# Eight-stage network on one core: an order written out as turns, softplus and decays kept in PSUM, one scan per state tile, double-width GpSimd products, stage 4's weights laid over the convolutions'

## The reference

```python
x = _layernorm(x + _L0_attn_ref(x, ...))   # stage 0: Mamba mixer and MLP
x = _layernorm(x + _L0_ffn_ref(x, ...))    # stage 1: 16-head attention, then 7 experts
x = _layernorm(x + _L1_attn_ref(x, ...))   # stage 2: linear attention
x = _layernorm(x + _L1_ffn_ref(x, ...))    # stage 3: MLP with binarized weights
x = _layernorm(x + _L2_attn_ref(x, ...))   # stage 4: 16-head attention
x = _layernorm(x + _L2_ffn_ref(x, ...))    # stage 5: 8 experts
x = _layernorm(x + _L3_attn_ref(x, ...))   # stage 6: attention with a pruned context
x = _layernorm(x + _L3_ffn_ref(x, ...))    # stage 7: 8 experts and a shared one
```

```python
xs, zs = jnp.split(jnp.einsum('bld,ed->ble', x, in_proj_w), 2, axis=-1)
u  = jax.nn.silu(conv(xs)); zc = jax.nn.silu(conv(zs))
dt, Bm, Cm = jnp.split(jnp.einsum('bld,ed->ble', u, x_proj_w), [...], axis=-1)
delta = jax.nn.softplus(jnp.einsum('blr,dr->bld', dt, dt_proj_w) + dt_proj_b)
dA = jnp.exp(delta * A)          # decays, A = -exp(A_log)
dBu = delta * Bm * u
h = dA_t * h + dBu_t             # scan over the tokens
y = einsum(h, Cm) + u * Dp
x = x + einsum(concat(y, zc), out_proj_w)
x = x + gelu(ln(x) @ w1 + b1) @ w2 + b2
```

## Time and profile before

| | |
|---|---|
| median of 3 runs | 1385.8 us |
| the profiled execution, its own time | 1385.3 us |
| its span, first to last instruction | 1383.5 us |
| TensorE busy | 1280.2 us (93%) |
| VectorE busy | 941.4 us (68%) |
| ScalarE busy | 896.0 us (65%) |
| GpSimd busy | 789.7 us (57%) |
| mean granted TensorE clock | 0.968 |
| DMA, mean | 49 GB/s |

### The profile page before, as it was taken

How to read it: one execution, slowest core, us unless ns; L and a number is a source line. 1 busy time by engine, 2 the same in 40 slices (tenths; PEclk the granted TensorE clock), 3 DMA queues, 4 the chain that set the end, 5 groups by cost and what they waited for, 6 DMA issues and landing times.

```text
span 1383.5 us, 26286 instructions
## 1 busy us (share of the span) xinstructions
PE 1280.2 (93%) x8734; PEld 909.6 (66%) x8734; DVE 941.4 (68%) x3661; ACT 896.0 (65%) x2495; POOL 789.7 (57%) x876
## 2 busy tenths in 40 slices
PE   8577988899977889999999999999999999999997
PEld 4233655567644666677767867777777867886665
DVE  5989868677568677757563663485988659864253
ACT  6736689787474679767787676556568664775231
POOL 2998666576378556466556756355435325450534
PEclk9868899899998999999999999999999999999999
DMA  8742000101141100110010001301020030001431
GB/s 285 193 122 76 9 9 2 55 2 55 55 103 28 37 1 1 55 65 1 1 63 1 1 1 63 125 1 62 2 81 1 1 93 1 2 2 70 115 91 32
DMA packets 23109, 67.86 MB, mean 49 GB/s; under 512 B 2336, under 2 KB 9120, under 8 KB 20672
## 3 DMA queue, kind: packets, MB, share of 16 engines
q1 hardware_dynamic: 22976, 66.20, 15.2%
HBM read 62.85 MB, written 3.34 MB: 48 GB/s over the span
## 4 chain that ended last, share of the span: by engine, by line
PE 65%; DVE 11%; POOL 9%; ACT 8%; issue 5%; DMA 2%; SPq 0%; POOLq 0%; DVEq 0%; ACTq 0%
PE bank L1064 57%; PE bank L1068 8%; ACT arena L1514 6%; POOL arena L2315 3%; DMA arena<-cf 2%; DVE arena L1769 2%; DVE arena L2261 2%; POOL arena L2386 1%; DVE arena L2254 1%; DVE arena L2012 1%; POOL arena L2385 1%; POOL arena L2328 1%; DVE arena L1947 1%; DVE arena L2010 1%; DVE stats L1783 1%
## 5 line engine op out<-in xcount | busy, mean ns | idle before, releaser
L1514 ACT ACTIVATE arena<-arena 128x256 f32<-128x256 f32 (+4 forms) x808 | 357.9, 447 | 64.7 <-DVE arena L2012 32.5
L1514 ACT ACTIVATE arena<-bank 128x512 f32<-128x512 f32 (+3 forms) x355 | 190.7, 563 | 230.3 <-PE bank L1064 144.5
L1064 PE MATMUL bank<-XT,W 128*128 128x512 f32 (+1 forms) x752 | 290.2, 523 | 1.0 <-DVE arena L1775 0.6
L1064 PEld LDWEIGHTS bank<-W,arena 128*128 128x128 f32 x1888 | 231.5, 193 | 52.5 <-issue 39.4
L1064 PE MATMUL bank<-W,arena 128*128 128x128 f32 (+1 forms) x1888 | 243.4, 279 | 6.2 <-POOL arena L2328 3.1
L2385 POOL TENSOR_TENSOR arena<-arena 128x256 f32<-128x256 f32 x192 | 117.6, 613 | 220.8 <-DVE arena L2018 220.0
L1064 PE MATMUL bank<-arena 128*32 128x128 f32 (+8 forms) x2912 | 228.0, 336 | 16.2 <-ACT arena L1514 7.4
L2328 POOL TENSOR_TENSOR arena<-arena 128x512 f32<-128x512 f32 (+1 forms) x108 | 170.8, 1601 | 93.7 <-DVE arena L1769 39.0
L1064 PEld LDWEIGHTS bank<-arena 128*32 128x32 f32 (+4 forms) x2912 | 154.8, 153 | 81.1 <-issue 45.2
L1068 PE MATMUL bank<-CF,arena 128*128 128x128 f32 x1312 | 182.1, 279 | 23.9 <-POOL arena L2386 10.7
L2386 POOL TENSOR_TENSOR arena<-arena 128x512 f32<-128x512 f32 x192 | 199.7, 1040 | 0.0
(11 more groups left out here) (138 smaller groups left out, 1700.5 us busy)
## 6 DMA issues: line engine op xcount, KB each, us to landing
arena<-rws SPq DMA_DIRECT2D x8, 2048.0 KB, 7.4
arena<-rep SPq DMA_DIRECT2D x62, 256.0 KB, 5.9
arena<-rws SPq DMA_DIRECT2D x4, 1792.0 KB, 6.6
W<-w SPq DMA_DIRECT2D x2, 2124.0 KB, 8.6
arena<-rws SPq DMA_DIRECT2D x8, 384.0 KB, 10.4
W<-w SPq DMA_DIRECT2D x1, 2692.0 KB, 9.3
XT<-wkq SPq DMA_DIRECT2D x4, 512.0 KB, 8.3
W<-w SPq DMA_DIRECT2D x1, 2005.0 KB, 15.5
```

The lines of the kernel that those rows point to most:

```text
L1064: return e.matmul(o, lhsT, rhs, start=start, stop=stop, skip_group_check=True)
L1514: return e.activation(o, a, func, **kw)
```

## The change

It has seven parts.

1. The order is no longer computed by priorities. A table `TURNS` gives every part of every step a place in one sequence of about 3,900 (a negative number chooses the second of two engines); each engine's list is that sequence cut down to its parts. The tables `AHEAD`, `URGENT`, `HASTE` and `STAY` go.
2. Softplus works in the bank of `0.dt`: the exponential, the three corrections and delta itself stand in PSUM. A new ScalarE step `0.dc` copies delta to SBUF for `0.da`, without the first column of each sequence, which VectorE sets to zero. `0.da`'s exponentials leave that column out too, so that its decay is zero.
3. With a zero decay at the first token of each sequence, one scan runs over all 512 columns.
4. `0.db` multiplies two ring tiles in one GpSimd operation, 128x1024.
5. `0.da` repeats two tiles at a time in two banks, not four in four: eight groups a chunk for four. C stays in its bank until the last `0.ac`, and VectorE's `0.hc` reads it there; GpSimd still reads a copy in SBUF.
6. `0.b` and `0.x` go. b2 comes into `0.o`'s bank by four matmuls with one row, and `0.y` gets a second VectorE operation that leaves 2x + y where `0.o` adds.
7. Stage 0's weights change places, stage 4's go to columns 2087 to 4519, over the projections and taps, and its `load` waits for `0.in#1` and `0.dt` of all chunks, not for `0.e`. In addition, a `1.km` step is whole on ScalarE, or its second half on either engine.

```diff
-W_AT = {3: WMAX - 1160, 2: WMAX, 4: 2048}
+W_AT = {3: WMAX - 1160, 2: WMAX, 4: 4135}
...
-    loads = [("load", s, 0, [("f" if q else "0.e", 0, c, q) for q in OVER[s] for c in range(NC)]
+    loads = [("load", s, 0, [need for q in OVER[s] for c in range(NC) for need in ([("f", 0, c, q)] if q else [("0.in", 1, c, 0), ("0.dt", 0, c, 0)])]
...
+TURNS = {
+    ("0.n", 0, 0): (9, 13, 14, 16, 18), ("0.in", 0, 0): (25, 33, 53, 66), ("0.bc", 0, 0): (40, 47), ("0.dt", 0, 0): (43, 52, 59),
...
+        for p, (engines, one, other) in enumerate(x.parts):
+            turn = next(rows[x.name, x.s, x.c])
+            x.parts[p] = (engines[0], one) if turn > 0 else (engines[1], other)
+            turns[x.parts[p][0]].append((abs(turn), x, p))
...
+        def later(a):
+
+            return a.rearrange("p (b l) -> p b l", b=2)[:, :, 1:256]
...
                     act(s0(c, 12), bank[b.i][:, :], ACT.Abs, bias=wt(0, "dtb")).then_inc(has["sf_a"], 1)
...
-                    act(s0(c, 13), s0(c, 12), ACT.Exp, scale=-1.0).then_inc(has["sf_e"], 1)
+                    act(bank[b.i][:, :], s0(c, 12), ACT.Exp, scale=-1.0).then_inc(has["sf_e"], 1)
                     act(s0(c, 4), s0(c, 12), ACT.Tanh, scale=0.5).then_inc(has["sf_t"], 1)
+                elif name == "0.dc":
+                    b = u("b", "0.dt", c)
+                    on.wait_ge(*after("du", "0.du", c))
+                    act(later(step0(c, 0)), later(bank[b.i][:, :]), ACT.Copy).then_inc(done[b.i], 1)
...
-                    ts(s0(c, 14), s0(c, 13), 1.0, None, ALU.add).then_inc(has["sf_f"], 1)
+                    ts(s0(c, 14), ps[:, :], 1.0, None, ALU.add).then_inc(has["sf_f"], 1)
...
-                    own(tt(step0(c, 0), s0(c, 13), s0(c, 12), ALU.add))
-                    on.wait_ge(*own.last())
-                    tt(step0(c, 1), step0(c, 0), s0(c, 6), ALU.mult).then_inc(has["du"], 1)
+                    own(e.memset(step0(c, 0).rearrange("p (b l) -> p b l", b=2)[:, :, 0:1], 0.0))
+                    own(tt(ps[:, :], ps[:, :], s0(c, 12), ALU.add))
+                    on.wait_ge(*own.last())
+                    tt(step0(c, 1), ps[:, :], s0(c, 6), ALU.mult).then_inc(has["du"], 1)
...
-                    own(e.tensor_tensor_scan(h[:, 0:256], bank[a.i][:, 0:256], h[:, 0:256], 0.0, ALU.mult, ALU.add))
-                    e.tensor_tensor_scan(h[:, 256:512], bank[a.i][:, 256:512], h[:, 256:512], 0.0, ALU.mult, ALU.add
-                                         ).then_inc(done[a.i], 1)
+                    e.tensor_tensor_scan(h, bank[a.i][:, :], h, 0.0, ALU.mult, ALU.add).then_inc(done[a.i], 1)
...
-                    tt(ring0(c, n), ring0(c, n), s0(c, 16), ALU.mult).then_inc(has["hc_v"], 1)
+                    tt(ring0(c, n), ring0(c, n), bank[cc.i][:, :], ALU.mult).then_inc(has["hc_v"], 1)
...
-                    e.tensor_tensor(h, h, s0(c, 8), ALU.mult).then_inc(has["dB"], 1)
+                    e.tensor_tensor(h, h, s0(c, 8).unsqueeze(1).to_broadcast([128, 2, 512]), ALU.mult).then_inc(has["dB"], 1)
...
+                    if s == 0:
+                        for j in range(4):
+                            mm(ps[:, j * 128:(j + 1) * 128], cst("one", 1), wt(0, "b2", 0, 1), j == 0, False)
```

More of the change, by code:

```diff
@@ L267, in stage_steps @@
             add("0.h", j, ("0.m", 0))
-        add("0.x", 0, ("0.m", 0), ("0.b", 0, PREP))
-        add("0.o", 0, ("0.x", 0), *[("0.h", j) for j in range(4)])
+        add("0.o", 0, *[("0.h", j) for j in range(4)])
         add("0.e", 0, ("0.o", 0))
@@ L489, in __init__ @@
         self.parts, self.at = parts_of(name, n), 0
-        self.open, self.tail, self.since, self.behind = 0, 0.0, LANDS.get((name, c), 0.0), []
+        self.open, self.since, self.behind = 0, LANDS.get((name, c), 0.0), []
 def order_of_steps():
@@ L559, in opened @@
         return out + [(r, last, f, g) for r, o, last, f, g in HELD.get((x.name, x.n), ()) if o == x.at]
[L561 to L562 removed]
+    while any(turns.values()):
         best = None
         for g in "PAVGD":
[L565 to L581 removed]
+            _, x, p = turns[g][0] if turns[g] else (0, None, 0)
+            if x is None or x.open or x.at != p:
+                continue
+            t, k = max(x.since, free[g]), len(opened(x))
+            if k > len(banks):
+                continue
+            if k:
+                t = max(t, sorted(banks)[k - 1][0])
+            if best is None or t < best[0]:
+                best = t, g, x
+        t, g, x = best
+        turns[g].pop(0)
         if g == "A" and x.name in TABLE:
@@ L606, in order_of_steps @@
         if x.at < len(x.parts):
-            offer(end + HOP[g], x)
+            x.since = end + HOP[g]
         else:
-            left -= 1
             for y in x.behind:
@@ L1615, in _ @@
                     on.wait_ge(*filled(a))
-                    act(bank[a.i][:, :], bank[a.i][:, :], ACT.Exp, scale=am[:, g:g + 1], bias=am[:, 16 + g:17 + g]).then_inc(has["dA"], 1)
+                    act(later(bank[a.i][:, :]), later(bank[a.i][:, :]), ACT.Exp, scale=am[:, g:g + 1], bias=am[:, 16 + g:17 + g]).then_inc(has["dA"], 1)
                 elif name == "0.h":
@@ L1961, in _ @@
                     on.wait_ge(*filled(b))
-                    tt(s0(c, 2), bank[b.i][:, :], rows(0, c), ALU.add).then_inc(done[b.i], 1)
+                    own(tt(s0(c, 2), bank[b.i][:, :], rows(0, c), ALU.add))
+                    stt(rows(0, c), rows(0, c), 2.0, bank[b.i][:, :], ALU.mult, ALU.add).then_inc(done[b.i], 1)
                 elif name == "0.m":
```

220 lines of the change are left out of this document (91 added, 129 removed), and 371 rows, old and new, of tables (AHEAD, EMITS, HASTE, OPENS).

## The result

The changed kernel takes 1339.7 us, the median of 4 runs (1338.38 to 1341.19). The ratio to the kernel before is 0.9666, with a 95% interval from 0.9646 to 0.9686: 3.3% faster, some 46 us. The prediction was 1352, with a range from 1325 to 1378. The profiled execution took 1339.95 us, 1.8 more than its span of 1338.2.

What follows compares the result with a forecast made beforehand. TensorE was taken as the bound after 525 us, other engines in earlier stretches. Terms -22 - 7 - 12 + 7.3 + 0.5 = -33.2 took the span from 1383.5 to 1350.3, the median to 1352; range 1325 to 1378.

Steps and rivals of the forecast that it cites:

- the gain of the first stretch: Stages 0 of c0, c1, c2, 31 to 165 us: 22 us shorter, between GpSimd's 10.7 and VectorE's 24.4.
- What bounds the kernel: TensorE bounds from 525 us on; VectorE and GpSimd bound 31 to 165 us, ScalarE 165 to 300.
- So this goes with the idle time.: TensorE's clock fell where it had been idling, costing 32.5 us in three stretches, 19.7 of it from 31 to 165.
- The products by B: GpSimd in the three stages 0: 46 products at 1502 ns become 23 wide ones at 2365, -14.7 us.
- the 4 us put on such catches: Stages 0: by the skill's rule, ten VectorE operations caught by wide products cost some 4 us more, making the sum 1356.
- 385 to 525 us: c3's stage 0 with stage 4 of c0 starting earlier: 12 us won, bounds 0 and 22.
- After 525: TensorE is the bound there with 12.2 us idle: no change.
- TensorE's work: Pairs for fours, bias matmuls and form changes: +7.3 us to the sum, with 12.2 more covered by idle time.
- 165 to 300: Attention of stage 1, limited by ScalarE: 7 us won of 24.6 idle and clock, bounds 0 and 15.
- the higher price that the prediction weighed: ScalarE's table loads: about 2.66 us a switch by the skill, not 1.28; the sum would be 1359.
- Rival C: Slower, 1399 us: twice as many groups of decays could double TensorE's 17.3 us of waits for scans; chance 0.08.
- B: Rival: the order packs better, 40 us idle and 12 for the clock stay, 1328.5 us (1315 to 1335); chance 0.15.

Runs made afterwards that it cites:

- after: The changed kernel itself, all seven parts and the new order, against the kernel before: 1339.7 us, ratio 0.9666.
- ninth run: The kernel before with all its own operations, but its parts in the changed kernel's sequence: 1381.4 us, ratio 0.9960 to the kernel before.
- second run: The changed kernel with two scans a tile, single products by B, VectorE's product by C from SBUF and softplus corrections in SBUF as before: 1354.8 us.
- twelfth run: The changed kernel with each double product by B made as two of 128x512 in the same place: 1339.9 us.
- third run: The changed kernel with stage 4 of c0 held back behind the last step of c3's stage 0: 1357.8 us.

## Why the prediction was right, and where it wasn't

By its number it was right, 12 us too high; by its steps it was half right. That the number came so near is in part luck: the gain of the first stretch was taken 13 us too large, and against that stand the gains of the other stretches, 22 too small, and the new work, 4 too large.

**What bounds the kernel.** Held: all that was gained is TensorE's idle time and clock, 60 us, less 15 of new work. That VectorE and GpSimd are the bound of the three stages 0 held for before. In after neither is: the landmark, stages 0 over by 143, failed, for c1's last `0.ac` ended at 161.8 instead of 165.4. Two more signs failed with it: GpSimd above 90% there (110.6 of 134 is 83%) and a granted clock above 0.9 (0.85). The stretch gained because TensorE did more of other work in it (117.3 busy us for 98.7), not because it got shorter.

**"So this goes with the idle time."** This step on the clock failed. In the run with filled waits there was 7 us less idle time and no better clock; with full rows the clock came back. In this stretch the half clock goes with the 32-row form of these groups. Why it does was not found. The clock's cost stayed, 17.6 against 19.7, which is more than the 13.5 us that the first stretch gave less than forecast.

**The products by B.** The price of 1.502 us for a single product failed. The "-14.7" is a sum of two things: 23 x 2 x (1.502 - 1.270) = 10.7 for what held the singles up, 23 x (2.540 - 2.353) = 4.3 for the width. Of the 1.502 the new order alone took it to 1.407 (ninth run, all operations old), and VectorE's input in PSUM from some 1.40 (second run) to 1.270. The twelfth run shows the width to be worth nothing here. The mistake was to price an operation by a row in which another engine was holding it up, while the change also removed that engine's hold. The prediction had set the Trainium skill's rule from "SBUF — State Buffer", section "SBUF: two separate sides", against the wide products; the traces agree with it in direction, 2.569 us for a wide product with VectorE on SBUF against 2.349 with C in PSUM. But in after, where most of VectorE's operations around them read a bank, the wide product's mean was 2.353 us, so the 4 us put on such catches don't show. In the second run's remainder the same hold, taken away, is part of the 10 to 12 us.

**VectorE.** Prices right (0.674 for 0.686, corrections 2.2 us for 2.1). The one scan is 1.213 for 1.27, 0.06 saved for 0.1 taken.

**385 to 525 us.** Mis-sized: 20.8 for 12. The third run put 18 us on stage 4 of c0 standing there; the upper bound of 22 was nearer, as TensorE's work was there for the taking and no other engine was full (ScalarE, the busiest, 113.5 of 140).

**After 525.** "No change" failed, 9.6 us. The prediction had named it among what would make it wrong, the order without a price. In the ninth run it came with the order alone: 2.9 us idle there.

**TensorE's work.** +15.0 for +19.5. The 0.96 for a pair was read from the start of its weight loads to the next form, not from its matmuls; the pair takes 1.05 us, hardly less than a group of four (1.07), which makes the pairs +16.5 for +13.6. Eight bias passes take 1.05 for 1.0. So neither price was too high, and why the sum still came out smaller stays open.

**ScalarE.** 165 to 300 gave 10.8 for 7, and the table loads are 1.283 each. In after, too, the next operation starts 1.28 to 1.30 us after a load, so the higher price that the prediction weighed didn't come. Even seven fewer loads bought nothing.

**Adding the parts up.** The prediction gave each part a value of its own and took the order for what lets it through. The table of two by two shows that this step failed: the same parts are worth +36 in one order and -41 in the other. Rival C, slower because groups wait (1399), has its sign borne out by the parts in the old order (1422) but not its mechanism: TensorE's waits for scans were 14.8 us there, not double the 17.3, and its idle time fell; the loss was new work and the clock. In after the same waits fell to 4.7 us. B, that the order packs better, was right in kind: 45 us of idle time for its 40, but 23 of the clock's cost for its 12.

## What to carry to other kernels

Price an operation from a row in which nobody else holds it up, and ask which part of its time belongs to its neighbour: here GpSimd's product became faster when VectorE's operands moved to PSUM, and GpSimd's own remedy was worth nothing. When a change holds more of a scarce resource (banks) and rewrites the order, test both halves apart; a fixed order is fitted to its parts, and the change can win what neither half wins alone. Split TensorE's time into idle time, clock and work before naming a cause: in several runs here the clock made most of a difference that waits seemed to explain. Fill TensorE's idle stretches by making other chunks' work available there: idle time fell by 51 us, while stage 0 of the first three chunks ended only 3.6 us earlier.
